# Two sparse convolutions on one core: gathers and sums written out item by item

## The chip, the cores and the metric

One core of one Trainium2 chip runs one program. The metric is the device time of an execution in microseconds; the time before is the median of three runs.

## The reference, cut to what matters

Four blocks act one after the other on x, 6250 nodes of 256 float32 features, each added to x behind a layer norm: a sum over 106,250 weighted edges, a mixture of eight experts, a graph network of two convolutions, and a feed-forward block over selected tokens. The change touches the two convolutions only:

```python
def _gcn_conv(x, src, dst, W, b):
    ones = jnp.ones((src.shape[0],), x.dtype)
    deg_out = jnp.maximum(segment_sum(ones, src, num_segments=N), 1.0)
    deg_in = jnp.maximum(segment_sum(ones, dst, num_segments=N), 1.0)
    h = x * (deg_out ** (-0.5))[:, None]
    h = h @ W
    m = segment_sum(h[src], dst, num_segments=N)
    return m * (deg_in ** (-0.5))[:, None] + b
h = _gcn_conv(x, src, dst, W1, b1)
h = relu(h)
h = _gcn_conv(h, src, dst, W2, b2)
h = _layer_norm(h, gamma, beta)
```

The edges come sorted by their target dst. All tensors are float32.

## The kernel before, in words

**Tiles.** The nodes lie in T = 49 tiles of 128. The edges are cut into NI = 880 items of up to 128 edges whose targets all lie in one tile of nodes. For each item three tables in SBUF hold a column of 128 entries: SRCI the source rows, DREL the place of each target within its tile, and (in the first stage) weights. The array `rows` holds for each item the column in `reg_b` at which its tile's sums begin. A convolution first sums the gathered rows and only then multiplies by W, tile by tile.

**One item of a convolution.** (1) POOL issues an indirect DMA that gathers 128 rows of 256 features from DRAM (`conv_rows` in the profile) into a slot of a ring of U = 16 in `work` (L535, in `gathers`). (2) DVE compares IOTA, a row of 0 to 127, with the item's column of DREL and so writes a one-hot matrix of 128x128 (L1153, in `item_sums`). (3) PE multiplies the one-hot by the gathered rows and a column of ones into a PSUM bank, 257 columns: the sums over the targets, and their number (L1617, in `item_products`). (4) DVE adds the bank to the accumulator in `reg_b`, at a column that comes from a register (L1165).

**The rings.** The slot of a gather is free when the matmul sixteen items back is done: POOL waits on `p1_mm` (`p2_mm` in the second pass). There are four one-hots and four banks. DVE makes the one-hot of item i+2 in front of the accumulation of item i; PE waits for the accumulation of item i-4 before it writes its bank again. Each gather counts up `ring_dma0` to `ring_dma15`.

**Index columns.** POOL doesn't read its index column from the table. ACT copies eight columns at a time to the staging array STG (L685, in `staging`), when the eight gathers before them in those slots have landed, and POOL waits for this copy once in eight gathers. Before each gather POOL increments a semaphore `turn` and waits for `const`.

**Loops.** All four engines run over the items in a hardware loop of 16 items a round, with the first round written out; what they wait for is a register plus a constant. DVE loads the offsets of four items into registers at a time (L257, in `load_offsets`) and computes further addresses in its sequencer (the profile's DVEq).

**The order around the passes.** The engines work in the order of their own programs and meet at semaphores. Before the first pass stands the mixture of experts (L1482 is one of its matmuls), after it the products with W1: PE transposes and multiplies each tile (L1520 in `tile_products`), DVE scales it and adds the bias (L1285, in `product`), ACT applies the relu, SP writes the rows out, and the second pass begins. POOL, behind its last gather of the first pass, adds a row of constants to all of X (L567, 128x12544 elements), and then turns to the second pass. DVE, behind its last accumulation of a pass, takes a maximum and inverse roots of the counts before the first `product`.

**Other lines that the rows name.** L468: eight gathers of edge blocks at the start, one behind the other with no wait between them, the index columns in an array `small`. L481: the scatter of the first stage's messages, in a loop of 880. L889 and L1019: tensor_tensor compares of two SBUF operands in other stages. L977: a one-hot of the first stage, the same form as L1153.

Of the kernel before, what the change touches and what calls it, by code (L numbers as in the profile page):

```python
# [14 lines left out]
P = 128  # L15
ALU = mybir.AluOpType
# [37 lines left out]
def gnn_program(nc, x, src, dst, edge_weight, Wr, br, ln_g, ln_b, W1, b1, W2, b2,  # L54
# [31 lines left out]
    with ExitStack() as ctx:  # L86
# [77 lines left out]

        G, OH, OHT = carve(0, U * W, 4 * P, 2 * P)
# [47 lines left out]
        STG, PIDX = sm(U).bitcast(I32), sm(U).bitcast(I32)  # L213
# [125 lines left out]
        def _(sp):  # L339
# [72 lines left out]
            sp.wait_ge(z("p2_add"), NI + 1)  # L412
            sp.wait_ge(z("p2_stg"), NI)
# [18 lines left out]
        def _(pool):  # L432
# [91 lines left out]
            def gathers(tag, table):  # L524

                def body(i0, first):
                    for u in range(U):
                        if u % 8 == 0:
                            pool.wait_ge(z(f"{tag}_stg"), i0 + u + 8)
                        if not first:  # L530
                            pool.wait_ge(z(f"{tag}_mm"), i0 + u + 1 - U)
                        if u % 8 == 0 or not first:
                            pool.sem_inc(z("turn"), 1)
                        pool.wait_ge(z("const"), CONST)
                        g.indirect_dma_start(G[:, u, 0:D], None, table,  # L535
                                             bass.IndirectOffsetOnAxis(ap=STG[:, u:u + 1], axis=0)
                                             ).then_inc(z(f"ring_dma{u}"), 16)
                body(0, True)
                with pool.Fori(U, NI, U) as i0:
                    body(i0, False)  # L540
# [49 lines left out]
        def _(act):  # L590
# [87 lines left out]
            def staging(tag):  # L678

                def body(i0, first):  # L680
                    for h in range(0, U, 8):
                        if not first:
                            for u in range(h, h + 8):
                                act.wait_ge(z(f"ring_dma{u}"), i0 + BEFORE[tag])
                        a.copy(STG[:, h:h + 8], SRCI[:, bass.ds(i0 + h, 8)]).then_inc(z(f"{tag}_stg"), 8)  # L685
                body(0, True)
                with act.Fori(U, NI, U) as i0:
                    body(i0, False)

# [33 lines left out]
            staging("p1")  # L723
# [11 lines left out]
            staging("p2")  # L735
# [23 lines left out]
        def _(v):  # L759
# [390 lines left out]
            def item_sums(tag):  # L1150

                def onehot(i, j):
# [3 lines left out]
                def body(i0):  # L1156
                    for u in range(U):
                        i = i0 + u
                        if u % 4 == 0:
                            offs = load_offsets(DVE_, ROW_D, i, (T - 1) * (D + 1))  # L1160
# [533 lines left out]
```

## Time and profile before

| what | value |
| --- | --- |
| time, median of 3 runs | 5863.63 us (5860.67 to 5864.42) |
| the profiled execution: span | 6669.2 us |
| instructions in it | 93083 |
| items of the two passes | 2 x 880 |

The profile comes from one execution that was recorded by the hardware profiler; its own time is its span, and it is longer than the timed executions, which run without a recording. PE is TensorE's matmuls, PEld its weight loads, DVE VectorE, ACT ScalarE, POOL GpSimd, SP SyncE. A name ending in q is the sequencer of that engine: register arithmetic, branches and register loads are put there and are not counted as busy time. PEclk is the clock that the throttle granted to TensorE, as a share of 2.4 GHz.

### The profile page before, as it was taken

Reading aid. Unit: us, or ns where it says so; the run is one execution under the profiler, and the core shown is the slowest. Engines: PE = TensorE matmul, PEld = TensorE weight load, DVE = VectorE, ACT = ScalarE, POOL = GpSimd, SP = SyncE. Lnnn points to the kernel's source line nnn. Section 1 sums busy time; section 2 is a strip of 40 time slices with the busy share of each in tenths; the row PEclk is TensorE's granted clock in tenths of the full one; section 3 lists DMA queues with packets and bytes.
Section 4 is the critical chain, followed back from the end, with each engine's and each line's share of the span. In section 5 each row is a group of like instructions: output and inputs, shape, how many; then the busy total and the mean of one; then the engine's idle time right before and its main releaser. Section 6 shows DMA issues by size and latency. Waiting matters only on the chain. (4 is left out here: it accounts for less than half of the span.)

```text
span 6669.2 us, 93083 instructions
## 1 busy us (share of the span) xinstructions
PE 4350.5 (65%) x15535; PEld 2796.3 (42%) x15536; DVE 3245.9 (49%) x12513; ACT 1175.7 (18%) x3960; POOL 3014.1 (45%) x2954
## 2 busy tenths in 40 slices
PE   1667677777677759999945555555555555555459
PEld 0444444444455446666633233332333323323346
DVE  7555555555566664333334444444544444444662
ACT  4333333333000053222220000000110000000322
POOL 0555555555000012333336666666546666666412
PEclk9777677667999959999976766666776776676769
DMA  2122222222666651221243333333232333333211
GB/s 69 70 75 72 73 74 75 74 73 73 183 186 188 178 179 25 33 33 33 33 121 87 86 87 88 87 87 87 70 94 87 88 88 88 87 87 88 72 41 31
DMA packets 287945, 575.13 MB, mean 86 GB/s; under 512 B 57794, under 2 KB 138307, under 8 KB 287758
## 3 DMA queue, kind: packets, MB, share of 16 engines
q0 software_dynamic: 152576, 376.72, 19.9%
q1 hardware_dynamic: 101902, 136.46, 6.5%
q10 hardware_dynamic: 33408, 61.31, 3.3%
q8 instruction: 19, 0.31, 0.0%
q14 instruction: 40, 0.33, 0.0%
HBM read 408.39 MB, written 173.72 MB: 87 GB/s over the span
## 5 line engine op out<-in xcount | busy, mean ns | idle before, releaser
L1617 PE MATMUL bank<-work 128*128 128x257 f32 x3520 | 1453.6, 552 | 1283.1 <-DVE work L1153 727.1
L535 POOL DMA_INDIRECT work<-conv_rows,small x1760 | 1666.2, 947 | 1088.0 <-issue 417.9
L1617 PEld LDWEIGHTS bank<-work 128*128 128x128 f32 x3520 | 806.2, 261 | 1930.6 <-DVE work L1153 921.5
L1165 DVE TENSOR_TENSOR reg_b<-reg_b,bank 128x257 f32 x1760 | 743.2, 422 | 915.6 <-issue 435.6
L481 POOL DMA_INDIRECT messages<-work,small x880 | 857.4, 974 | 687.6 <-DVE small L998 258.4
L1482 PE MATMUL bank<-reg_b,work 128*128 x1760 | 885.8, 598 | 4.3 <-ACT work L627 0.5
L1153 DVE TENSOR_SCALAR work<-iota,tables 128x128 f32<-128x128 f32 x1764 | 556.2, 316 | 623.4 <-issue 577.8
L1498 PE MATMUL bank<-work,reg_b 128*128 128x257 f32 x1856 | 474.6, 408 | 192.5 <-DVE reg_b L1019 192.4
L685 ACT COPY small<-tables 128x8 int32 (+1 forms) x220 | 43.2, 197 | 2557.2 <-DMA work<-conv_rows,small 2377.8
L637 ACT COPY work<-bank 128x256 f32<-128x256 f32 x880 | 329.1, 374 | 909.5 <-PE bank L1482 526.6
L1498 PEld LDWEIGHTS bank<-work,reg_b 128*128 128x128 f32 x1856 | 332.0, 196 | 335.5 <-issue 283.1
L1461 PE MATMUL bank<-small,trib 128*128 128x49 bf16 x1761 | 229.9, 215 | 348.0 <-DVE small L993 317.1
L993 DVE SCALAR_TENSOR_TENSOR small<-bank,small 128x49 f32<-128x49 f32 x880 | 184.9, 210 | 501.1 <-remote 385.6
L1461 PEld LDWEIGHTS bank<-small,trib 128*128 128x128 bf16 x1761 | 201.8, 128 | 523.8 <-DVE small L993 375.8
L665 ACT ACTIVATE work<-bank,param_t 128x128 f32<-128x128 f32 x1056 | 286.5, 382 | 753.2 <-PE bank L1564 753.1
L1482 PEld LDWEIGHTS bank<-reg_b,work 128*128 128x128 f32 x1760 | 384.0, 271 | 26.4 <-issue 10.1
L1556 PE MATMUL bank<-reg_b,work 128*128 x1696 | 385.5, 381 | 2.5 <-ACT work L665 2.5
L1546 PE MATMUL bank<-reg_a,work 128*128 x848 | 383.4, 595 | 1.1 <-DVE work L1093 1.1
L1452 PE MATMUL bank<-ident,work 128*128 128x128 f32 x881 | 322.9, 367 | 90.3 <-issue 60.1
L496 POOL DMA_INDIRECT work<-expert_in_rows,work x106 | 104.4, 985 | 555.8 <-DVE work L1085 537.1
L977 DVE TENSOR_SCALAR work<-iota,tables 128x128 f32<-128x128 f32 x881 | 321.1, 365 | 26.8 <-issue 20.2
L1556 PEld LDWEIGHTS bank<-reg_b,work 128*128 128x128 f32 x1696 | 315.2, 191 | 42.3 <-issue 3.5
(297 smaller groups left out, 4566.3 us busy)
## 6 DMA issues: line engine op xcount, KB each, us to landing
work<-messages SPq DMA_DIRECT2D x232, 258.0 KB, 3.0
work<-messages ACTq DMA_DIRECT2D x232, 258.0 KB, 3.3
work<-conv_rows,small POOLq DMA_INDIRECT x1760
messages<-work,small POOLq DMA_INDIRECT x880
conv_rows<-work SPq DMA_DIRECT2D x14, 896.0 KB, 4.1
reg_a<-in_L_ffn_W_dram SPq DMA_DIRECT2D x8, 1024.0 KB, 12.7
reg_b<-in_L_ffn_W_dram SPq DMA_DIRECT2D x8, 1024.0 KB, 12.2
residual_rows<-reg_a SPq DMA_DIRECT2D x7, 896.0 KB, 4.6
```

Of the source, the lines that this page charges most:

```text
L481: g.indirect_dma_start(msgs, bass.IndirectOffsetOnAxis(ap=PIDX[:, u:u + 1], axis=0), G[:, u, :], None, bounds_check=E - 1, oob_is_err=Fals ...
L535: g.indirect_dma_start(G[:, u, 0:D], None, table, bass.IndirectOffsetOnAxis(ap=STG[:, u:u + 1], axis=0)).then_inc(z(f"ring_dma{u}"), 16)
L637: a.copy(G[:, u, 0:D], ps[3 + u % 2][:, 0:D]).then_inc(z("m_row"), 1)
L1153: v.tensor_scalar(OH[:, j % 4, :], IOTA[:], DREL[:, bass.ds(i, 1)], None, ALU.is_equal).then_inc(z(f"{tag}_oh"), 1)
L1165: v.tensor_tensor(acc, acc, ps[u % 4][:, 0:D + 1], ALU.add).then_inc(z(f"{tag}_add"), 1)
L1452: pe.transpose(ps[j % 2][:, 0:P], OH[:, j % 4, :], IDENT[:]).then_inc(z("m_tr"), 1)
L1461: ins = pe.matmul(ps[2][:, 0:T], TRIB[:, which, :], BOH[:, j % 4, 0:T], start=False, stop=False, skip_group_check=True)
L1482: pe.matmul(ps[3 + u % 2][:, 0:D], OHT[:, u % 2, :], XNf[:, bass.ds(offs[u % 4], D)], start=True, stop=True).then_inc(z("m_mm"), 1)
L1498: pe.matmul(ps[u // 2 % 4][:, 0:D + 1], SOH[:, u % 8, :], G[:, u, 0:D + 1], start=(u % 2 == 0), stop=(u % 2 == 1)).then_inc(z("s_mm"), 1)
L1546: ins = pe.matmul(ps[1 + h // 512][:, :], XE[:, s, c, :], w_, start=(c == 0), stop=(c == KC - 1))
L1556: ins = pe.matmul(ps[5 + s][:, 0:D], HTS[:, k, :], w_, start=(k == 0), stop=(k == HC - 1))
L1617: pe.matmul(ps[u % 4][:, 0:D + 1], OH[:, u % 4, :], G[:, u, 0:D + 1], start=True, stop=True).then_inc(z(f"{tag}_mm"), 1)
```

## The change

Only the two convolution passes change.

- POOL: the gathers of all 880 items are written out, with constants in place of registers. The index column is read from the table SRCI; there is no staging array, no `turn`, and no wait for `const`.
- ACT: the copies to the staging array are gone.
- DVE: the one-hots of four items are made by one tensor_tensor (IOTA repeated four times against four columns of DREL, each repeated over 128 elements) into a ring of eight one-hots, which lies in a part of `reg_a`. Those of items i+4 to i+7 stand in front of the accumulation of item i, where i is a multiple of four. Registers are loaded for sixteen items at a time. All items are written out.
- PE: all items are written out; eight banks in place of four; it waits once in four items for one-hots, and for the accumulation eight items back.
- The count `p1_add` starts at 0 in place of 1, so waits for its end ask for NI.

```diff
--- before.py
+++ after.py
@@ -162,6 +162,8 @@
         HID, HIS = (a_.bitcast(BF16) for a_ in (HIB[:, 0:EC // 2], HIB[:, EC // 2:EC]))
         CMPD, CMPS = CMPD.bitcast(BF16), CMPS.bitcast(BF16)
 
+        OHN = 4
+        OHP = ta[:, 0:2 * OHN * P].rearrange("p (s n) -> p s n", n=P)
         G, OH, OHT = carve(0, U * W, 4 * P, 2 * P)
         G = G.rearrange("p (u w) -> p u w", w=W)
         OH = OH.rearrange("p (s n) -> p s n", s=4)
@@ -210,7 +212,7 @@
             taken[0] += n
             return small[:, taken[0] - n:taken[0]]
         BOH = sm(4 * 26).bitcast(BF16).rearrange("p (s n) -> p s n", s=4)
-        STG, PIDX = sm(U).bitcast(I32), sm(U).bitcast(I32)
+        PIDX = sm(U).bitcast(I32)
         POS, JUNK = sm(4), sm(64)
         CNT = sm(104)
         ZERO = sm(2 * NT)
@@ -409,8 +411,7 @@
                 sp.wait_ge(z("relu1"), (c + 1) * CH)
                 sp.dma_start(nodes(conv2_t, c), XR[:, c % 2, :, :]).then_inc(z(f"rows_out{c % 2}"), 16)
 
-            sp.wait_ge(z("p2_add"), NI + 1)
-            sp.wait_ge(z("p2_stg"), NI)
+            sp.wait_ge(z("p2_add"), NI)
             sp.dma_start(fw1s[:, :, :], fw1.rearrange("(c p) h -> p c h", p=P)).then_inc(z("fw_in"), 16)
             sp.dma_start(fw2s[:, :, :], fw2.rearrange("(c p) d -> p c d", p=P)).then_inc(z("fw_in"), 16)
 
@@ -523,21 +524,13 @@
 
             def gathers(tag, table):
 
-                def body(i0, first):
-                    for u in range(U):
-                        if u % 8 == 0:
-                            pool.wait_ge(z(f"{tag}_stg"), i0 + u + 8)
-                        if not first:
-                            pool.wait_ge(z(f"{tag}_mm"), i0 + u + 1 - U)
-                        if u % 8 == 0 or not first:
-                            pool.sem_inc(z("turn"), 1)
-                        pool.wait_ge(z("const"), CONST)
-                        g.indirect_dma_start(G[:, u, 0:D], None, table,
-                                             bass.IndirectOffsetOnAxis(ap=STG[:, u:u + 1], axis=0)
-                                             ).then_inc(z(f"ring_dma{u}"), 16)
-                body(0, True)
-                with pool.Fori(U, NI, U) as i0:
-                    body(i0, False)
+                for i in range(NI):
+                    u = i % U
+                    if i >= U:
+                        pool.wait_ge(z(f"{tag}_mm"), i + 1 - U)
+                    g.indirect_dma_start(G[:, u, 0:D], None, table,
+                                         bass.IndirectOffsetOnAxis(ap=SRCI[:, i:i + 1], axis=0)
+                                         ).then_inc(z(f"ring_dma{u}"), 16)
 
             def chunk(c):
                 w_ = slice(c * CH, (c + 1) * CH)
@@ -674,18 +667,6 @@
                 with act.Fori(2, tiles, 2) as j0:
                     for s in range(2):
                         hidden(j0 + s, e_(j0 + s), False)
-
-            def staging(tag):
-
-                def body(i0, first):
-                    for h in range(0, U, 8):
-                        if not first:
-                            for u in range(h, h + 8):
-                                act.wait_ge(z(f"ring_dma{u}"), i0 + BEFORE[tag])
-                        a.copy(STG[:, h:h + 8], SRCI[:, bass.ds(i0 + h, 8)]).then_inc(z(f"{tag}_stg"), 8)
-                body(0, True)
-                with act.Fori(U, NI, U) as i0:
-                    body(i0, False)
 
             def evacuate(tag, t):
 
@@ -720,7 +701,6 @@
                     if c >= 3:
                         act.wait_ge(*rows_out((c - 1) % 2, 1, (c - 1) // 2))
                     ln_apply("ln3", c - 1, lambda i: X[:, (c - 1) * CH + i, :], lambda i: XR[:, (c - 1) % 2, i, :])
-            staging("p1")
             inv_root("di", RM)
             evacuate("c1", 0)
             for t in range(T):
@@ -732,7 +712,6 @@
                     act.wait_ge(*rows_out(c % 2, 2, c // 2))
                 a.activation(XR[:, c % 2, t % CH, :], ZB[:, t % 2, :], ACT.Relu, scale=DO[:, t:t + 1]
                              ).then_inc(z("relu1"), 1)
-            staging("p2")
 
             evacuate("c2", 0)
             for t in range(T):
@@ -1149,28 +1128,26 @@
 
             def item_sums(tag):
 
-                def onehot(i, j):
-                    v.tensor_scalar(OH[:, j % 4, :], IOTA[:], DREL[:, bass.ds(i, 1)], None, ALU.is_equal
-                                    ).then_inc(z(f"{tag}_oh"), 1)
-
-                def body(i0):
-                    for u in range(U):
-                        i = i0 + u
-                        if u % 4 == 0:
-                            offs = load_offsets(DVE_, ROW_D, i, (T - 1) * (D + 1))
-                        onehot(i + 2, u + 2)
-                        v.wait_ge(z(f"{tag}_add"), i + 1)
-                        v.wait_ge(z(f"{tag}_mm"), i + 1)
-                        acc = ACCf[:, bass.ds(offs[u % 4], D + 1)]
-                        v.tensor_tensor(acc, acc, ps[u % 4][:, 0:D + 1], ALU.add).then_inc(z(f"{tag}_add"), 1)
-                step(v.memset(G[:, :, D:D + 1], 1.0))
-                onehot(0, 0)
-                onehot(1, 1)
-                v.engine_nop().then_inc(z(f"{tag}_add"), 1)
-                with v.Fori(0, NI - U, U) as i0:
-                    body(i0)
-                body(NI - U)
-
+                def onehots(i):
+                    if i >= 2 * OHN:
+                        v.wait_ge(z(f"{tag}_mm"), i - OHN)
+                    v.tensor_tensor(OHP[:, i % (2 * OHN):i % (2 * OHN) + OHN, :],
+                                    IOTA[:].rearrange("p (o n) -> p o n", o=1).to_broadcast([P, OHN, P]),
+                                    DREL[:, i:i + OHN].rearrange("p (s o) -> p s o", o=1).to_broadcast([P, OHN, P]),
+                                    ALU.is_equal).then_inc(z(f"{tag}_oh"), OHN)
+
+                v.memset(G[:, :, D:D + 1], 1.0).then_inc(z(f"{tag}_one"), 1)
+                onehots(0)
+                for i in range(NI):
+                    if i % U == 0:
+                        offs = load_offsets(DVE_, ROW_D, i, (T - 1) * (D + 1), U)
+                    if i % OHN == 0 and i + OHN < NI:
+                        onehots(i + OHN)
+                    v.wait_ge(z(f"{tag}_mm"), i + 1)
+                    if i:
+                        v.wait_ge(z(f"{tag}_add"), i)
+                    acc = ACCf[:, bass.ds(offs[i % U], D + 1)]
+                    v.tensor_tensor(acc, acc, ps[i % 8][:, 0:D + 1], ALU.add).then_inc(z(f"{tag}_add"), 1)
 
             v.wait_ge(z("s_add"), NIS + 1)
             step(v.tensor_scalar(DI, ACC[:, :, D], 1.0, None, ALU.max))
@@ -1274,7 +1251,7 @@
                 v.wait_ge(*rows_out(k, 1))
             v.engine_nop().then_inc(z("conv_ready"), 1)
             item_sums("p1")
-            v.wait_ge(z("p1_add"), NI + 1)
+            v.wait_ge(z("p1_add"), NI)
             step(v.tensor_scalar(RM, ACC[:, :, D], 1.0, None, ALU.max))
             inv_root("di", DI, RM)
 
@@ -1293,7 +1270,7 @@
             v.wait_ge(z("acc2_zero"), 1)
             v.engine_nop().then_inc(z("conv_ready"), 1)
             item_sums("p2")
-            v.wait_ge(z("p2_add"), NI + 1)
+            v.wait_ge(z("p2_add"), NI)
 
             for t in range(T):
                 product("c2", 1, t, ACC[:, t, 0:D], GB2B).then_inc(z("lin2"), 1)
@@ -1607,18 +1584,17 @@
                               stop=(n == steps - 1), skip_group_check=True).then_inc(z(f"{tag}_inv"), 1)
 
             def item_products(tag):
-                def body(i0, first):
-                    for u in range(U):
-                        i = i0 + u
-                        pe.wait_ge(z(f"{tag}_oh"), i + 1)
-                        pe.wait_ge(z(f"ring_dma{u}"), i0 + (16 + BEFORE[tag]))
-                        if not (first and u < 4):
-                            pe.wait_ge(z(f"{tag}_add"), i - 2)
-                        pe.matmul(ps[u % 4][:, 0:D + 1], OH[:, u % 4, :], G[:, u, 0:D + 1], start=True, stop=True
-                                  ).then_inc(z(f"{tag}_mm"), 1)
-                body(0, True)
-                with pe.Fori(U, NI, U) as i0:
-                    body(i0, False)
+
+                pe.wait_ge(z(f"{tag}_one"), 1)
+                for i in range(NI):
+                    u = i % U
+                    if i % OHN == 0:
+                        pe.wait_ge(z(f"{tag}_oh"), i + OHN)
+                    pe.wait_ge(z(f"ring_dma{u}"), 16 * (i // U + 1) + BEFORE[tag])
+                    if i >= 8:
+                        pe.wait_ge(z(f"{tag}_add"), i - 7)
+                    pe.matmul(ps[i % 8][:, 0:D + 1], OHP[:, i % (2 * OHN), :], G[:, u, 0:D + 1], start=True, stop=True
+                              ).then_inc(z(f"{tag}_mm"), 1)
 
 
             pe.wait_ge(z("par_in"), PAR_IN)
@@ -1641,14 +1617,14 @@
             pe.wait_ge(z("conv_ready"), 1)
             item_products("p1")
             pe.wait_ge(z("tail_in"), 8 * 16)
-            pe.wait_ge(z("p1_add"), NI + 1)
+            pe.wait_ge(z("p1_add"), NI)
             for t in range(T):
                 if t >= 4:
                     pe.wait_ge(z("lin1"), t - 3)
                 tile_products("c1", t, D, lambda c: gws[:, 0, c, :], 2 + t % 4, 0)
             pe.wait_ge(z("conv_ready"), 2)
             item_products("p2")
-            pe.wait_ge(z("p2_add"), NI + 1)
+            pe.wait_ge(z("p2_add"), NI)
             for t in range(T):
                 if t >= 4:
                     pe.wait_ge(z("lin2"), t - 3)
```

## Rows read from the trace of the kernel before

**Rows 1.** Page, part 1: busy time, share and instructions of each engine.

```profile
PE 4350.5 (65%) x15535; PEld 2796.3 (42%) x15536; DVE 3245.9 (49%) x12513; ACT 1175.7 (18%) x3960; POOL 3014.1 (45%) x2954
```

**Rows 2.** Stages: stretch, us; busy PE, PEld, DVE, ACT, POOL; clock; DMA; GB/s.

```profile
2525.00:3400.00 875.00, 860.27 (x3638) 596.12 (x3636) 314.77 (x882) 241.05 (x881) 271.42 (x212) 0.99 0.20 32
...
3454.00:4772.00 1318.00, 719.99 (x1738) 399.46 (x1738) 545.68 (x1735) 21.32 (x108) 832.52 (x880) 0.68 0.30 87
```

**Rows 3.** Page, part 5: costliest groups; busy, mean ns; idle before.

```profile
L535 POOL DMA_INDIRECT work<-conv_rows,small x1760 | 1666.2, 947 | 1088.0 <-issue 417.9
...
L481 POOL DMA_INDIRECT messages<-work,small x880 | 857.4, 974 | 687.6 <-DVE small L998 258.4
...
L1153 DVE TENSOR_SCALAR work<-iota,tables 128x128 f32<-128x128 f32 x1764 | 556.2, 316 | 623.4 <-issue 577.8
```

**Rows 4.** Timeline of POOL: start, duration (us), instruction, wait before it.

```profile
3454.46 1.03 POOL L535 DMA_INDIRECT work<-conv_rows,small  x1 [42.38 <-DMA conv_rows<-work]
...
3455.79 0.99 POOL L535 DMA_INDIRECT work<-conv_rows,small  x1 [0.30 <-issue]
...
4627.01 0.94 POOL L535 DMA_INDIRECT work<-conv_rows,small  x1 [3.34 <-PE bank L1617]
...
4771.35 0.94 POOL L535 DMA_INDIRECT work<-conv_rows,small  x1 [0.30 <-issue]
...
4772.31 22.41 POOL L567 TENSOR_TENSOR reg_a<-reg_a,reg_b 128x12544 f32<-128x12544 f32 x1
...
4874.39 0.96 POOL L535 DMA_INDIRECT work<-conv_rows,small  x1 [79.66 <-DMA conv_rows<-work]
...
6187.77 0.95 POOL L535 DMA_INDIRECT work<-conv_rows,small  x1 [0.30 <-issue]
```

**Rows 5.** Timeline of DVE inside the first pass.

```profile
4617.80 0.42 DVE L1165 TENSOR_TENSOR reg_b<-reg_b,bank 128x257 f32 x1 [0.35 <-PE bank L1617]
...
4626.42 0.42 DVE L1165 TENSOR_TENSOR reg_b<-reg_b,bank 128x257 f32 x1 [2.70 <-PE bank L1617]
```

**Rows 6.** DVE's sequencer at L1153, two stretches: least, median, most ns.

```profile
L1153 DVEq FUSED_REGOPS  x11: 64/64/102, 4608.1 to 4616.8; - x11
...
L1153 DVEq FUSED_REGOPS  x2: 700/712/724, 4621.9 to 4625.5; - x2
```

**Rows 7.** Timeline of POOL at the start.

```profile
118.67 2.01 POOL L468 DMA_INDIRECT reg_b<-edge_blocks,small  x1 [0.30 <-issue]
```

**Rows 8.** Single lines: count, then least, median, most ns, and when.

```profile
L1019 DVE TENSOR_TENSOR reg_b<-iota,small x464: 426/427/430, 1677.8 to 2332.4; 128x256 f32<-128x256 f32 x155
...
L889 DVE TENSOR_TENSOR reg_a<-ident,small x5: 1202/1203/1226, 112.3 to 148.3; 128x1024 f32<-128x1024 f32 x5
...
L257 DVEq TENSOR_LOAD <-rows x110: 1823/1828/1874, 1701.3 to 2318.4; - x110
...
L1617 PE MATMUL bank<-work x3520: 377/602/797, 3457.4 to 6197.1; 128*128 128x257 f32 x196
```

**Rows 9.** Timeline of DVE at the start of the first pass.

```profile
3460.43 0.28 DVE L1153 TENSOR_SCALAR work<-iota,tables 128x128 f32<-128x128 f32 x1
```

**Rows 10.** Timeline of DVE at the start.

```profile
118.65 1.20 DVE L889 TENSOR_TENSOR reg_a<-ident,small 128x1024 f32<-128x1024 f32 x1
```

**Rows 11.** Timeline of POOL and DVE in the message stage.

```profile
1403.24 1.04 POOL L481 DMA_INDIRECT messages<-work,small  x1 [0.30 <-DVE small L998]
...
1403.09 0.34 DVE L977 TENSOR_SCALAR work<-iota,tables 128x128 f32<-128x128 f32 x1
```

**Rows 12.** Timeline of DVE at the ends of the passes.

```profile
4772.96 0.42 DVE L1165 TENSOR_TENSOR reg_b<-reg_b,bank 128x257 f32 x1 [1.82 <-PE bank L1617]
...
4773.30 21.52 DVE L1153 TENSOR_SCALAR work<-iota,tables 128x128 f32<-128x128 f32 x1
...
4806.51 0.48 DVE L1285 SCALAR_TENSOR_TENSOR work<-bank,small,reg_b 128x256 f32<-128x256 f32 x1 [0.27 <-PE bank L1520]
...
6197.77 0.42 DVE L1165 TENSOR_TENSOR reg_b<-reg_b,bank 128x257 f32 x1
```

## The prediction

> **What bounds the kernel now.** I read the page first, then the stages one by one. The page shows a program of several stages in which no engine is busy throughout: PE 65%, DVE 49%, POOL 45% [rows 1]. The table by stage says where the change can act: the first convolution takes 1318 us, the second as long, and in the first PE is busy 720 us at a granted clock of 0.68, DVE 546, POOL 833, ACT 21 [rows 2]. The expert stage beside them has PE busy 860 of 875 us at clock 0.99 and isn't touched.
>
> The costliest groups give the work of one item of a convolution: one gather of 947 ns on POOL and one one-hot of 316 ns on DVE [rows 3], beside an accumulation of 0.42 us. None fills the 1.50 us that an item takes. POOL's own rows explain that. A gather follows the one before after 0.30 us whenever nothing holds it, so 1.25 us from start to start, and now and then POOL stops, here for 3.34 us, until a matmul has freed its slot [rows 4]. The passes run from their first gather to their last in 1316.9 and 1313.4 us [rows 4]; 879 steps of 1.25 us are 1098.8 us. So POOL's pace is 2198 us of the two, and the stops are 433 us.
>
> What stops POOL stands in DVE's rows of the same microseconds: from 4617.8 to 4626.4 DVE starts three accumulations of 0.42 us, the first and the last of them shown [rows 5], and its own sequencer instructions (register additions before a one-hot), 64 ns in the microseconds before, take 700 to 724 ns each [rows 6]. PE then waits for a one-hot and POOL for PE's matmul, whose end frees the slot.
>
> **POOL, part by part.** The semaphore increment, the wait for constants and the register arithmetic in front of each gather go. The eight gathers at L468 have nothing in front of them and still stand 0.30 us apart, as the one shown [rows 7]; so 1.25 us is the gather's own pace and this saves 0 us (from below, too: fewer instructions can't lengthen it; a written-out list costs at most what L468 shows). Reading the index column from the table instead of the staged copy: the nearest rows are the gathers at L468, whose index column lies in another place of the same kind, with the same 0.30 us, so 0. ACT's copies disappear, 21 us of its 1318 [rows 2]; POOL waits for one of them only before every eighth gather, and the copy is due as soon as the eight transfers of the round before have landed, so 0; what is late next in its place is the matmul fifteen items back, as now.
>
> **PE.** Waits on constants instead of registers and eight banks instead of four. PE is in use for 0.82 us per item [rows 2], under POOL's 1.25: 0 while POOL sets the pace; without that cover PE would have 0.43 us to spare per item.
>
> **DVE.** Four one-hots become one tensor_tensor of 128x512 with two operands in SBUF. That form stands in the trace: 427 ns for 256 columns, 1203 ns for 1024 [rows 8], so 1.01 ns a column and 0.69 us for 512, against 4 x 0.316 = 1.26 us. The offsets come 16 at a time instead of 4: 8 take DVE 1828 ns [rows 8], 0.23 us each, so 16 take about 3.6 us once in 16 items, the same per item (0.23). DVE needs 0.17 + 0.42 + 0.23 = 0.82 us per item instead of 0.97, both under 1.25. A pause of 3.6 us is three gathers; the ring holds 16 and item 1 was through DVE 4.6 us after its gather's start [rows 4, 9], so it is hidden. Fewer sequencer instructions per item (three or four instead of five) shorten the slow stretches where they occur.
>
> **The new cost.** POOL and DVE block each other in this trace. At L468 one gather of eight takes 2.01 us, where the median is 0.95. It started at 118.67, 0.02 us after a DVE tensor_tensor with two SBUF operands that ran until 119.85 [rows 7, 10]: 1.18 us were left, the gather got 1.06 longer. At 1403.24 a scatter took 1.04 us, where the mean is 0.97 [rows 3], while a one-hot had 0.19 us left [rows 11]. Both fit one reading: a gather that starts while such a DVE instruction runs is longer by what that has left, less 0.12 us. Today's one-hot of 0.28 us can add 0.16 us at most, and the mean gather of the passes is 947 ns [rows 3]: nothing. The new one lasts 0.69 us, 440 times. It starts right behind the accumulation of the item before: for item 1 that was 4.64 us after its gather's start [rows 4, 9], which is 0.89 us after a later gather's start, so it ends at 1.58, with the next gather at 1.25: 0.33 left, 0.21 added. At the low of PE's two clock levels, that is; at the high one a matmul takes 377 instead of 797 ns [rows 8], a pair of them and all behind it come about 0.6 us sooner, and nothing collides. A mean clock of 0.68 [rows 2] is 64% of the low level: 440 x 0.21 x 0.64 = 59 us. With no fixed phase the mean is 0.57 x 0.57 / (2 x 1.25) = 0.13 us, 57 us in all. Ends: 0 and 440 x 0.57 = 250 us. I take 55, where both readings meet.
>
> The Trainium skill, "SBUF — State Buffer", section "Who interferes with whom", says that a tensor_tensor with both inputs in SBUF contends with GpSimd's reads, but infers that it does not hold up descriptor generation, which needs the write side. The row at 118.67 speaks against that inference; by it the new cost would be 0 and the time 5841 us (the second case below).
>
> **The ends of the passes.** After the last gather of pass 1 POOL adds beta for 22.4 us, and DVE's next one-hot takes 21.5 us instead of 0.28: it gets through only when POOL is done [rows 4, 12]. The items still due follow, and the first product comes at 4806.5 [rows 12]. Afterwards the last one-hots are made eight items earlier and an accumulation passes beside POOL (0.42 us at 4772.96 [rows 12]). The maximum and the roots may still wait for POOL, and take about 2.3 us: 4794.7 + 2.3 = 4797.0, 9.5 us saved. Pass 2's last accumulation starts 10.0 us after its last gather [rows 4, 12], where 4.3 would do (4.64 less the 0.34 between accumulation and one-hot): 5.7. Together 15 us where DVE lags as in the profile, 2.5 where it doesn't; I take 8.
>
> **The sum and the timed runs.** In the profiled execution: 6669.2 - 15 + 55 and minus whatever of the 433 us goes; I expect half, so about 6490. The timed median, 5863.6, is 805.6 us below that span. The expert stage (875 us, PE-bound) can't be shorter without the recording, and to find 805.6 us outside it and the convolutions, the remaining 3161 us would have to shrink by 25%. So at least part of the 433 us, and I think nearly all, is absent from the timed runs: the stretched sequencer instructions look like time that the recording costs. Bounds for the stops in the timed runs: 0 and 433; I take 15, near the lower. Timed: 5863.6 - 15 (stops) - 8 (ends) + 55 (collisions) = **5896 us**.
>
> **Rivals.**
> 1. *Collisions, as above*, 0.42: 5896, its own range 5865 to 5985.
> 2. *No collisions*, 0.26: the phase misses, or one long gather proves little. For it: the page's inference, and that one long gather is one. Against it: two separate places give the same 0.12 us. 5863.6 - 15 - 8 = 5841, half of the time inside the bound of no change.
> 3. *The stops are real in the timed runs and go*, 0.20; faster. Place: DVE's slow stretches. For it: they take 433 us of the profiled span, one-hots four at a time and eight banks let DVE and PE run ahead, and the sequencer has fewer instructions to be slow in. Against it: the 805.6 us above. Price: half of the stops real 5863.6 - 217 - 8 + 55 = 5694, all of them 5471. It decides as soon as more than 47 us of stops go.
> 4. *The slow stretches stay and the longer register load lands in them*, 0.12: then each load that falls into one (8.6 us of the 20 us that 16 gathers take, so 43% of 110) holds DVE, and so POOL, between 0 and 3.6 us longer; at the middle 47 x 1.8 = 85 us: 5981. This is also the case in which the change doesn't do what it says.
>
> **Numbers.** Range 5660 to 5985: cases 1, 2 and 4, and case 3 up to 250 us of real stops (5863.6 - 250 - 8 + 55). A difference under 0.2% (12 us) counts as none. Faster: nearly all of case 3 and half of case 2, 0.31. Same: half of case 2 and the low end of case 1, 0.23. Slower: 0.46.
>
> **What the profile afterwards would show.** Gathers with a mean above 0.97 us and some hundred between 1.0 and 1.5, each begun beside a 0.69 us tensor_tensor (case 1), or 0.946 throughout (case 2). The step from gather to gather still 1.25 us where nothing interferes; a shorter step would make the POOL part wrong. 440 one-hots of 0.69 us; register loads of 3.6 us with no stop of POOL behind them (else case 4). Stops of POOL below 220 us in sum; a time far below 5800 would mean that I was wrong to ascribe them to the recording. Pass 1's beta addition with accumulations done within 6 us of its start.

## The result, and the profile after

The changed kernel takes 5895.44 us (median of 4 runs, 5883.44 to 5898.29), the kernel before in the same session 5864.02 (5860.67 to 5866.95): ratio 1.0050, 95% interval 1.0038 to 1.0063. It is slower by 31 us; 5896 was forecast. The profiled execution is one of the four, 5883.44 us with a span of 5881.8.

Part 1 of the page of the changed kernel, and of its part 5 the groups of an item (line, engine, operation; busy us, mean ns):

```profile
PE 4671.4 (79%) x15535; PEld 2711.5 (46%) x15536; DVE 3117.7 (53%) x11189; ACT 1142.5 (19%) x3740; POOL 3045.6 (52%) x2954
...
L1596 PE MATMUL bank<-work,reg_a 128*128 128x257 f32 x3520 | 1920.6, 655 | 382.0 <-DMA work<-conv_rows,tables 222.7
L531 POOL DMA_INDIRECT work<-conv_rows,tables x1760 | 1695.1, 963 | 648.4 <-issue 419.6
...
L1150 DVE TENSOR_TENSOR reg_b<-reg_b,bank 128x257 f32 x1760 | 742.0, 422 | 870.1 <-PE bank L1596 802.7
...
L1134 DVE TENSOR_TENSOR reg_a<-iota,tables 128x512 f32<-128x512 f32 x440 | 302.1, 686 | 375.1 <-PE bank L1596 305.7
```

Its first convolution in the table by stage (the columns of [rows 2]):

```profile
3080.00:4195.00 1115.00, 965.05 (x1755) 411.36 (x1756) 497.30 (x1098) 0.00 (x0) 846.61 (x880) 0.59 0.36 104
```

Its timeline of POOL: the first gather, two neighbours inside the pass, the last gather, the addition, and the second pass (start, duration in us):

```profile
3080.55 1.48 POOL L531 DMA_INDIRECT work<-conv_rows,tables  x1 [41.47 <-DMA conv_rows<-work]
...
3301.24 0.95 POOL L531 DMA_INDIRECT work<-conv_rows,tables  x1 [0.30 <-issue]
3302.49 1.35 POOL L531 DMA_INDIRECT work<-conv_rows,tables  x1 [0.30 <-issue]
...
4194.29 0.95 POOL L531 DMA_INDIRECT work<-conv_rows,tables  x1 [0.30 <-issue]
4195.26 22.41 POOL L560 TENSOR_TENSOR reg_a<-reg_a,reg_b 128x12544 f32<-128x12544 f32 x1
4288.92 0.96 POOL L531 DMA_INDIRECT work<-conv_rows,tables  x1 [71.25 <-DMA conv_rows<-work]
...
5404.00 0.95 POOL L531 DMA_INDIRECT work<-conv_rows,tables  x1 [0.30 <-issue]
```

And of DVE, beside the long gather and at the ends of the passes:

```profile
3302.34 0.68 DVE L1134 TENSOR_TENSOR reg_a<-iota,tables 128x512 f32<-128x512 f32 x1
...
4199.73 0.42 DVE L1150 TENSOR_TENSOR reg_b<-reg_b,bank 128x257 f32 x1 [1.23 <-PE bank L1596]
4200.19 17.55 DVE L1255 TENSOR_SCALAR small<-reg_b 128x49 f32<-128x49 f32 x1
...
4220.60 0.48 DVE L1262 SCALAR_TENSOR_TENSOR work<-bank,small,reg_b 128x256 f32<-128x256 f32 x1 [1.08 <-PE bank L1497]
...
5409.66 0.42 DVE L1150 TENSOR_TENSOR reg_b<-reg_b,bank 128x257 f32 x1 [1.60 <-PE bank L1596]
```

The passes now run from first to last gather in 1113.7 and 1115.1 us. Against [rows 4] that looks like 400 us won, and the spans like 787 (6669.2 to 5881.8), while the timed runs say 31 us lost. So the profile before can't be set against this one as it stands. Within this one the reader sees three things. POOL no longer stops: inside a pass all gathers follow 0.30 us behind the one before. The mean gather has grown from 947 to 963 ns [rows 3]. The gather at 3302.49 takes 1.35 us; it started while the one-hot of 3302.34 had 0.54 us left (0.684 us long), and it is 0.41 us longer than 0.946. Such a meeting, a gather that starts while a DVE instruction still runs and gets longer by it, is called a collision below; the phase of a one-hot is how long after a gather's start it starts itself.

### The profile page after: what moved, and what is told of

It reads as the page before. It is cut to its first block and busy times, and to the rows that moved or that the text cites. A ratio compares the mean times of both kernels' runs of the same rounds, so it can differ in the third digit from the quotient of the medians.

```text
span 5881.8 us, 81790 instructions
## 1 busy us (share of the span) xinstructions
PE 4671.4 (79%) x15535; PEld 2711.5 (46%) x15536; DVE 3117.7 (53%) x11189; ACT 1142.5 (19%) x3740; POOL 3045.6 (52%) x2954
## 5 line engine op out<-in xcount | busy, mean ns | idle before, releaser
L1596 PE MATMUL bank<-work,reg_a 128*128 128x257 f32 x3520 | 1920.6, 655 | 382.0 <-DMA work<-conv_rows,tables 222.7
L531 POOL DMA_INDIRECT work<-conv_rows,tables x1760 | 1695.1, 963 | 648.4 <-issue 419.6
L1596 PEld LDWEIGHTS bank<-work,reg_a 128*128 128x128 f32 x3520 | 824.9, 288 | 1477.0 <-DMA work<-conv_rows,tables 1038.0
L1459 PE MATMUL bank<-reg_b,work 128*128 x1760 | 736.0, 506 | 0.4
L1134 DVE TENSOR_TENSOR reg_a<-iota,tables 128x512 f32<-128x512 f32 x440 | 302.1, 686 | 375.1 <-PE bank L1596 305.7
L1429 PE MATMUL bank<-ident,work 128*128 128x128 f32 x881 | 283.7, 322 | 171.9 <-DVE work L956 89.0
L1533 PE MATMUL bank<-reg_b,work 128*128 x1696 | 383.8, 379 | 2.5 <-ACT work L658 2.5
L956 DVE TENSOR_SCALAR work<-iota,tables 128x128 f32<-128x128 f32 x881 | 329.4, 374 | 26.4 <-issue 23.1
L1459 PEld LDWEIGHTS bank<-reg_b,work 128*128 128x128 f32 x1760 | 319.9, 227 | 32.1 <-issue 0.2
L1533 PEld LDWEIGHTS bank<-reg_b,work 128*128 128x128 f32 x1696 | 314.0, 190 | 41.8 <-issue 3.5
L1082 DVE COPY work<-bank 128x512 f32<-128x512 f32 x132 | 91.4, 692 | 422.1 <-PE bank L1523 422.1
L1429 PEld LDWEIGHTS bank<-ident,work 128*128 128x128 f32 x881 | 141.8, 161 | 342.9 <-DVE work L956 209.8
```

What stands on the lines that cost most here:

```text
L531: g.indirect_dma_start(G[:, u, 0:D], None, table, bass.IndirectOffsetOnAxis(ap=SRCI[:, i:i + 1], axis=0)).then_inc(z(f"ring_dma{u}"), 16)
L956: v.tensor_scalar(OH[:, j % 4, :], IOTA[:], DREL[:, bass.ds(i, 1)], WT[:, bass.ds(i, 1)], ALU.is_equal, ALU.mult).then_inc(z("m_oh"), 1)
L1134: v.tensor_tensor(OHP[:, i % (2 * OHN):i % (2 * OHN) + OHN, :], IOTA[:].rearrange("p (o n) -> p o n", o=1).to_broadcast([P, OHN, P]), DREL ...
L1429: pe.transpose(ps[j % 2][:, 0:P], OH[:, j % 4, :], IDENT[:]).then_inc(z("m_tr"), 1)
L1459: pe.matmul(ps[3 + u % 2][:, 0:D], OHT[:, u % 2, :], XNf[:, bass.ds(offs[u % 4], D)], start=True, stop=True).then_inc(z("m_mm"), 1)
L1533: ins = pe.matmul(ps[5 + s][:, 0:D], HTS[:, k, :], w_, start=(k == 0), stop=(k == HC - 1))
```

## Experiments

Each was timed beside the kernel before on one chip. The last column is POOL's busy time in the 1760 gathers less the 1664.9 us that they take in a profile of the kernel before without stops (e11, below). Up to 5 us of it are no collision. In the profiles of e1, e2, e3, e5 and e7 the median gather takes 0.949 us, in the others 0.946 or 0.947; e5 is the changed kernel again, so the 3 ns belong to the execution and not to an edit. In e1 three of 1760 gathers take more than 1.0 us.

| run | us | ratio to before, 95% interval | gathers beyond 1664.9 us |
| --- | --- | --- | --- |
| changed | 5895.4 | 1.0050 (1.0038 to 1.0063) | 30.2 |
| e1 POOL and ACT part only | 5860.2 | 0.9998 (0.9989 to 1.0007) | 5.1 |
| e2 four tensor_scalar one-hots | 5861.3 | 1.0002 (0.9993 to 1.0011) | 8.5 |
| e3 four at once, in loops | 5881.7 | 1.0035 (1.0023 to 1.0048) | 29.4 |
| e4 eight at once | 5950.2 | 1.0153 (1.0139 to 1.0167) | 90.8 |
| e5 changed, again | 5892.9 | 1.0055 (1.0041 to 1.0069) | 38.3 |
| e6 one-hots wait for a landing | 5876.3 | 1.0026 (1.0017 to 1.0035) | 25.0 |
| e7 changed, addition on DVE | 5870.9 | 1.0016 (1.0007 to 1.0025) | 38.5 |
| e8 e2 and e7 together | 5845.3 | 0.9972 (0.9962 to 0.9983) | 4.2 |
| e9 e6 with loads of four | 5861.8 | 1.0004 (0.9994 to 1.0013) | 6.1 |
| e10 changed, loads of four | 5886.3 | 1.0043 (1.0029 to 1.0057) | 27.4 |
| e11 before, again | 5860.6 | 0.9999 (0.9989 to 1.0008) | 0 |
| e12 before, addition on DVE | 5839.6 | 0.9963 (0.9950 to 0.9977) | 0.1 |

**The kernel before, once more (e11).**

> The kernel before, run and profiled once more. Theory (the slow stretches of DVE's sequencer and POOL's stops behind them, 433 us, are made by recording and aren't in the timed runs): the timed runs at 5861, and either the profiled execution is again some 800 us above them, with stops, or it has none this time and passes of 1102 us each at a span near 5860. Rival (the stops are in the timed runs too): a profile without them would be some 430 us below the timed runs.

This profile has a span of 5860.8 us (its own time 5862.45). Its page, its first convolution by stage, and the two parts of L1153, the second the additions in DVE's sequencer (least, median, most ns):

```profile
PE 4717.4 (80%) x15535; PEld 2719.9 (46%) x15536; DVE 3221.5 (55%) x12513; ACT 1190.1 (20%) x3960; POOL 3012.8 (51%) x2954
...
L535 POOL DMA_INDIRECT work<-conv_rows,small x1760 | 1664.9, 946 | 653.2 <-issue 490.0
```

```profile
3084.00:4184.00 1100.00, 963.30 (x1755) 408.10 (x1756) 551.73 (x1753) 21.33 (x108) 832.26 (x880) 0.58 0.37 105
```

```profile
L1153 DVE TENSOR_SCALAR work<-iota,tables x1764: 274/280/23217, 3083.5 to 5385.2; 128x128 f32<-128x128 f32 x196
L1153 DVEq FUSED_REGOPS  x1728: 57/64/64, 3084.7 to 5363.4; - x192
```

None of the 1728 sequencer instructions takes more than 64 ns, where [rows 6] had 700 and more. The end of the first pass, on POOL and on DVE:

```profile
4183.33 0.95 POOL L535 DMA_INDIRECT work<-conv_rows,small  x1 [0.30 <-issue]
4184.30 22.41 POOL L567 TENSOR_TENSOR reg_a<-reg_a,reg_b 128x12544 f32<-128x12544 f32 x1
4281.80 0.96 POOL L535 DMA_INDIRECT work<-conv_rows,small  x1 [75.09 <-DMA conv_rows<-work]
```

```profile
4183.59 23.22 DVE L1153 TENSOR_SCALAR work<-iota,tables 128x128 f32<-128x128 f32 x1 [0.60 <-issue]
...
4213.06 0.48 DVE L1285 SCALAR_TENSOR_TENSOR work<-bank,small,reg_b 128x256 f32<-128x256 f32 x1 [1.46 <-PE bank L1520]
```

The passes take 1099.3 and 1099.1 us: POOL's own pace, without a stop. So the 433 us of stops were in that one recorded execution; that the timed ones have none follows from their times, which are those of e11. Of the 808 us between the two spans 432 lie in the passes and 370 before them. What made that recording slow stays open; this one, recorded in the same way, isn't. From here on this is the profile of before. Set against it the changed kernel's differs so: passes +30.4 us; from the last gather of the first to the first gather of the second 94.6 in place of 98.5, -3.8; before the passes -3.5; behind them -2.1; in sum the 21.0 us between the two spans.

**One part alone (e1, e2, e3).** e1 takes the diff of `gathers` and drops `staging`, and leaves DVE and PE as before. e2 changes one instruction of the changed kernel:

```diff
-                    v.tensor_tensor(OHP[:, i % (2 * OHN):i % (2 * OHN) + OHN, :], ...
+                    for k in range(OHN):
+                        v.tensor_scalar(OHP[:, i % (2 * OHN) + k, :], IOTA[:], DREL[:, i + k:i + k + 1], None,
+                                        ALU.is_equal).then_inc(z(f"{tag}_oh"), 1)
```

e3 puts the tensor_tensor of four one-hots and the eight banks into the loops of the kernel before.

> Before, with only POOL's and ACT's part of the change: gathers written out, index column from the table, no staging; one-hots, banks and DVE's and PE's loops as before. Theory (the whole extra time of the change is 128x512 one-hots that hold up gathers, 30 us in the profile after; the written-out gathers cost and save nothing): 5864 us within 5, gathers 0.946 us with none above 1.1. Rival (the written-out gather list or the column read from the table costs the 31 us): 5895. Rival (removing increments and waits saves time on POOL): below 5850.

> The changed kernel with each group of four one-hots made by four tensor_scalar instructions (0.28 us, one SBUF operand of 128 columns each) in place of one tensor_tensor of 128x512; all else as changed. Theory (collisions): the 30 us go, 5865 us, or up to 9 us less, as the ends of the passes gain what the profile after shows; gathers mean 0.946. Rival (written-out code, or constant waits, cost): stays at 5895. Rival (DVE's longer time per item matters): above 5895.

> Before, with only the one-hots of four items at once and eight banks, DVE and PE still in loops, offsets still four at a time, POOL and ACT as before. Theory (collisions): 5895 us within 10, with some hundred long gathers, each longer by what is left of the one-hot less 0.127 us. Rival (writing out costs): 5864.

The one-hots and gathers on the page of e2, and the gathers of e3:

```profile
L531 POOL DMA_INDIRECT work<-conv_rows,tables x1760 | 1673.4, 951 | 649.0 <-issue 419.4
...
L1135 DVE TENSOR_SCALAR reg_a<-iota,tables 128x128 f32<-128x128 f32 x1760 | 390.8, 298 | 366.7 <-PE bank L1595 305.1
```

```profile
L537 POOL DMA_INDIRECT work<-conv_rows,small x1760 | 1694.3, 963 | 651.1 <-issue 497.8
```

e1 and e2 lie within 1 us of the kernel before (e2's gathers take 8.5 us more, and the stretch from pass to pass 3.4 less); e3, which has nothing written out but a first and a last round, has the long gathers (mean 963 ns, as the changed kernel) and 21 us of the loss. That settles what costs: the 128x512 tensor_tensor. The written-out lists, the constant waits and the column read from the table cost and save nothing that can be measured. It doesn't settle whether the length or the two operands in SBUF do it, since e2 takes away both at once.

Two fences of e2, POOL and then DVE, show that the one-operand form collides too:

```profile
5179.58 1.04 POOL L531 DMA_INDIRECT work<-conv_rows,tables  x1 [0.30 <-issue]
```

```profile
5178.94 0.87 DVE L1135 TENSOR_SCALAR reg_a<-iota,tables 128x128 f32<-128x128 f32 x4
```

The last of the four tensor_scalar one-hots runs from 5179.524 to 5179.803: 0.22 us were left at the gather's start, and the gather is 0.09 us longer than 0.949. In e2 85 gathers that began with more than 0.15 us of such a one-hot left got longer (the first gather of a pass left out), by the rest less 0.129 us in the middle, which is the same rule as for the tensor_tensor; in sum it makes 3.9 us. In e11 22 gathers did, for 1.0 us in sum. None was lengthened by more than 0.1 us; these one-hots are 0.28 us long.

e3 came out 13 us under its expectation. Its profiled execution, at 5887.16 us, is 25 above e11's with 29.4 of gather time.

**Its size (e4).** One number, `OHN = 8`.

> The changed kernel with the one-hots of eight items at once (128x1024, about 1.20 us, 220 times) and a ring of sixteen. Theory: with the starting phases that the profile after shows (middle 0.66 us behind a gather's start) a one-hot leaves 0.66 + 1.20 - 1.25 = 0.61 us over the next gather's start, so 0.48 us are added about 220 x 2 / 2 = 220 times a pass-pair: some 100 us in place of 30, 5965 us (range 5930 to 6000). Rival (a cost per one-hot instruction, which are halved): 5880. Rival (written-out code): 5895.

The two groups on its page, then one gather and, in the next fence, the one-hot beside it:

```profile
L531 POOL DMA_INDIRECT work<-conv_rows,tables x1760 | 1755.7, 998 | 648.8 <-issue 419.4
...
L1134 DVE TENSOR_TENSOR reg_a<-iota,tables 128x1024 f32<-128x1024 f32 x220 | 268.9, 1222 | 373.1 <-PE bank L1596 338.1
```

```profile
3309.41 1.54 POOL L531 DMA_INDIRECT work<-conv_rows,tables  x1 [0.30 <-issue]
```

```profile
3308.91 1.22 DVE L1134 TENSOR_TENSOR reg_a<-iota,tables 128x1024 f32<-128x1024 f32 x1
```

Half as many one-hots, less DVE time in sum (269 for 302 us), and 90.8 us of added gather time, as 215 of the 220 have more than 0.15 us left over a gather's start; the kernel is 89.9 us above the one before. 5965 was expected, 5950 measured. The one-hot above had 0.72 us left at 3309.41; the gather got 0.59 us longer.

**Its phase (e5, e6, e9, e10).** e5 is the changed kernel again. e6 adds a wait in front of the one-hots:

```diff
                     if i % OHN == 0 and i + OHN < NI:
+                        n = i + 1
+                        v.wait_ge(z(f"ring_dma{n % U}"), 16 * (n // U + 1) + BEFORE[tag])
                         onehots(i + OHN)
```

e9 is e6, and e10 the changed kernel, with `load_offsets` for four items instead of sixteen.

> The changed kernel once more, beside the next three. Its first four timed runs lay between 5883 and 5898 us and its profile at 5882; with the clean spans of the two kernels without collisions at 5862 to 5863, theory (collisions of 29 us in the profile) expects 5885 to 5895 and about 65 long gathers a pass. Rival (the timed runs hold 10 us more that the profile doesn't show): 5895 again with a span of 5882.

> The changed kernel with one wait more on DVE: the 128x512 one-hot in front of accumulation i also waits until gather i+1 has landed. In the profile after, a matmul that waits for its gather starts 2.75 to 2.85 us behind that gather's start, so 0.25 to 0.35 us behind a later gather's start; a one-hot of 0.68 us begun there ends at about 1.0, before the next gather at 1.25. Theory (only the phase decides): collisions gone with the same 440 instructions of the same length, 5862 us within 4, gathers mean 0.950. Rival (a long tensor_tensor costs POOL something wherever it stands, or the written-out code costs): as the changed kernel, 5885 to 5895. Rival (the added wait delays accumulations): above that.

> As e6_phase, with the offsets loaded four at a time, as before the change, in place of sixteen. In e6_phase the one-hots of items 16n and 16n+12 made 8 collisions for 2.2 us, those of items 16n+4 and 16n+8, which come right behind the 3.6 us load of sixteen offsets and the accumulations held up by it, 75 for 23.6 us. Theory (only the phase decides, and the load had displaced it): under 5 us of collisions left, 5862 us within 4. Rival (the wait on the landing doesn't set the phase, or four shorter loads displace as much as a long one): 5870 to 5880 as e6_phase.

> The changed kernel with the offsets loaded four at a time; no other edit. In the profile after, all four groups of a round collide, those away from the load too (13.1 of 29.7 us, at a middle phase of 0.71 us). Theory (the phase behind an accumulation makes collisions by itself): some 15 to 30 us stay, 5878 to 5895 us. Rival (the long load is the whole cause): 5862.

Gathers on the pages of e6, e9 and e10, and what ended DVE's idle time before the one-hots in e9:

```profile
L531 POOL DMA_INDIRECT work<-conv_rows,tables x1760 | 1689.9, 960 | 647.8 <-issue 411.8
```

```profile
L531 POOL DMA_INDIRECT work<-conv_rows,tables x1760 | 1671.0, 949 | 648.2 <-issue 425.2
```

```profile
L531 POOL DMA_INDIRECT work<-conv_rows,tables x1760 | 1692.3, 962 | 649.9 <-issue 436.6
```

```profile
L1134 DVE TENSOR_TENSOR reg_a<-iota,tables x440: 691/693/755, 3079.8 to 5373.8; 128x512 f32<-128x512 f32 x147
...
  DMA work<-conv_rows,tables: 233.5, 234
```

e6 missed its 5862: the wait set the phase of the one-hots of items 16n and 16n+12 only (8 collisions in 220). The others start behind the load of sixteen offsets (median 3.59 us, the row further on) and the accumulations that it held up, when the landing is long past. e9 shortens the load, and with the same 440 tensor_tensor of 0.69 us the time is that of the kernel before: 5861.8. They still add 6 us of gather time, which the 4.5 us that it gains from pass to pass nearly make up. e10 has the short loads without the wait: 27 us stay. So the same number of instructions of the same length costs 6 us or 27; what costs is the part of them that lies over a gather's start. Without the wait the 440 one-hots make 98 (e10) to 145 (e5) gathers of more than 1.0 us, with it and the short loads 29 (e9).

e5's profiled execution took 5902.90 us, its others 5889 to 5900. Of the 19.5 us between its span (5901.3) and that of the first profile 8.1 are gather time (3.5 of them from a median gather of 949 in place of 947 ns), the rest lies outside the passes. The time varies from execution to execution: the changed kernel's nine runs spread over 19 us, those of the kernel before on one chip over some 8 to 11.

The register load of the changed kernel (least, median, most ns):

```profile
L259 DVEq TENSOR_LOAD <-rows x110: 3581/3590/3609, 3080.5 to 5386.8; - x110
```

**The addition on POOL (e7, e8, e12).** The line at L567 of the kernel before goes, and DVE gets one instruction in the loop of products:

```diff
-            g.tensor_tensor(X, X, per_column(BETB, T), ALU.add).then_inc(z("beta_in"), 1)
...
                 product("c1", 0, t, ZB[:, t % 2, :], GB1B).then_inc(z("lin1"), 1)
+                v.tensor_tensor(X[:, t, :], X[:, t, :], BETB, ALU.add).then_inc(z("beta_in"), 1)
```

> The changed kernel with POOL's 22.4 us addition behind pass 1 taken off POOL: DVE adds the row to one tile of X (128x256, 0.43 us, two SBUF operands) behind each of the 49 products, where it idles 0.6 to 0.9 us a tile. Theory (the addition locks DVE's maximum for 17.5 us at the end of pass 1): from the last accumulation to the first product about 4.5 us in place of 20.9, so 16 us less than the changed kernel in the same session. Rival (something else ends there anyway, such as rows or tail parameters, or the added DVE work slows the products): within 5 us of the changed kernel.

> Both repairs: four tensor_scalar one-hots per group (as in e2_ts_onehots) and the addition on DVE (as in e7_beta_on_dve); else the changed kernel. If both are independent: 5861 - 16 = 5845 us, faster than the kernel before by 0.27% and than the changed one by some 45 us. If the addition doesn't matter: 5861.

> The kernel before with one edit: POOL's 22.4 us addition behind pass 1 goes to DVE, one tile of 256 columns behind each of the 49 products (as in e7_beta_on_dve and e8_ts_and_beta). In the clean profile of the kernel before it holds the last one-hots for 23.2 us, and from the last gather of pass 1 to the first of pass 2 pass 98.5 us; with the addition moved e8_ts_and_beta has 78.5. Theory: 20 us less, 5841 us (range 5838 to 5847), so nothing of the change is needed for the fastest version. Rival (the shortening needs the written-out passes, where all one-hots are done before the addition): 5850 or more.

The last gather of pass 1 and the first of pass 2 in e12, then its DVE at that place:

```profile
4183.31 0.95 POOL L535 DMA_INDIRECT work<-conv_rows,small  x1 [0.30 <-issue]
4261.13 0.94 POOL L535 DMA_INDIRECT work<-conv_rows,small  x1 [76.88 <-DMA conv_rows<-work]
```

```profile
4188.62 0.42 DVE L1162 TENSOR_TENSOR reg_b<-reg_b,bank 128x257 f32 x1 [0.71 <-PE bank L1615]
4189.07 0.20 DVE L1275 TENSOR_SCALAR small<-reg_b 128x49 f32<-128x49 f32 x1
...
4192.53 0.48 DVE L1282 SCALAR_TENSOR_TENSOR work<-bank,small,reg_b 128x256 f32<-128x256 f32 x1 [1.46 <-PE bank L1518]
4192.93 0.42 DVE L1287 TENSOR_TENSOR reg_a<-reg_a,reg_b 128x256 f32<-128x256 f32 x1
```

From pass to pass 77.8 us instead of 98.5. The one-hot that e11 shows held for 23.22 us isn't held any more, and the maximum, 17.55 us long beside the addition in the changed kernel, takes 0.20. e7 gained 22 us on e5 (16 expected), e8 reached its 5845, and e12, the kernel before with this edit alone, is the fastest: 5839.6 us, 22 us under the kernel before beside it and, by the ratios, some 50 under the changed one. Of the 5.7 us between e8 and e12 4.1 are gather time.

## Why the prediction was right, and where only the sum was

**Right.** POOL sets the pace; 1.25 us is the gather's own (1.250 to 1.251 us a step in e11 and e12, so 1099 a pass; 1098.8 was worked out). The cover over PE is thinner than I read from [rows 2]: in e11 PE is in use for 963 us of a pass, 1.09 us per item and not 0.82, which leaves it 0.16 us and not 0.43. The POOL part is worth 0 (e1). The stops belong to one recorded execution: I put 15 of 433 us into the timed runs; e11 shows none, and e1, which leaves DVE's program as it was, is equal to before within 0.1%. Rival 3 falls (its price for all of the stops should read 5478 by the sum as given, not 5471), and rival 4 with it: the load of sixteen takes the 3.6 us foreseen, and no gather in the profile after waits more than 0.35 us for anything.

The rule of the collision held better than its two rows promised. Of the 179 gathers that began with more than 0.15 us of a one-hot left, the added time was that rest less 0.127 us in the middle, and less 0.124 to 0.131 in eight of ten (0.12 was read from two). Two of them, begun within 0.02 us of the one-hot's start, took no harm, and the one-hot grew by 0.04 to 0.06 us instead; for the tensor_scalar one-hots of e2 this is so up to 0.08 us behind their start, so that the 0.16 us that I took as the most one could add was 0.09. Rival 2 falls. The Trainium skill, "SBUF — State Buffer", section "Who interferes with whom", reports a probe in which a tensor_tensor did not stall DMAs, and infers that descriptor generation needs the write side, which it doesn't take. In this trace 177 of those 179 gathers were held up.

**Mis-sized.** The steps of the sum that failed are its terms for collisions, stops and ends: all three were off, and their errors nearly cancelled; that 5896 lies half a microsecond from the median is partly luck, as the executions themselves differ by 19 us:

| term | forecast, us | profiles show |
| --- | --- | --- |
| collisions | +55 | +30 (e5: 38, of which 5 are the 3 ns on every gather) |
| ends of the passes | -8 | -3.8 at the first, 0 at the second |
| stops in the timed runs | -15 | 0 |
| sum | +32 | +26; the spans differ from e11's by +21 and (e5) +40; timed +31.4 |

Between the +26 and the spans stand the stretches before and behind the passes, -5.6 us in the first profile and +5.5 in e5; no edit explains them.

The step on collisions failed twice in its detail. The phase: I carried item 1's accumulation (0.89 us behind a gather's start) over to all one-hots; they spread over the period, about half of them at 0.6 to 0.9 us. And the clock: "at the high one nothing collides" is wrong. Of the 90 one-hots that began when the matmul started last was one of less than 460 ns, 32 made a long gather, 8.4 us in sum. The granted clock in the pass was 0.59, and not 0.68 [rows 2]; e11, the same program as in [rows 2] without the stops, has 0.58, with PE busy 963 of 1100 us in place of 720 of 1318. With 0.59 the first reading would have given 440 x 0.21 x 0.82 = 76 us, still further off; that the two readings met near 55 was chance. With no phase assumed the second reading gave 57 us, twice what was found. The phases aren't spread evenly: e6 shows that the one-hots behind the load and the others have phases of their own. Why they lie so that half of the 57 us comes out isn't worked out.

The ends: in e11 DVE doesn't lag as in [rows 12], so the case of 2.5 us was the one that held. From the last gather of pass 1 to the first product pass 29.7 us in e11 and 26.3 after, 3.4 less; pass 2's last accumulation starts 5.5 us behind its last gather in e11 and 5.7 after, where [rows 4, 12] had 10.0, so nothing was to be had there. I took 8, between the two. What I saw there and didn't follow up, POOL's addition that locks DVE for 22 us, was worth 22 us (e12), the most of anything tried.

## What to carry to other kernels

Where GpSimd's gathers set the pace, look at what of a VectorE instruction lies over the next gather's start: that is what it costs here, not its own length. Keep such instructions short (the 0.28 us tensor_scalar added 0.09 us at most), or anchor them to an event with a known phase, and don't make them longer by merging. Whether a tensor_scalar of 0.69 us would have cost less than the tensor_tensor of 0.69 us was not run. Don't make GpSimd do a long elementwise pass where VectorE's next small step ends a stage. And set a profile's span beside the timed runs first: where they are as far apart as the 800 us here, stops seen in it have to be found in a second profile before they are worth a change.

## What the runs showed of the hardware

- VectorE and GpSimd hold each other up, both ways. A gather is held by the rest of a 0.68 us tensor_tensor less 0.127 us, and by the rest of a 0.28 us tensor_scalar less 0.129 us (e2). A 22.4 us GpSimd tensor_tensor holds a VectorE tensor_scalar over 49 columns for 17.55 us and a one-hot for 23.2 us.
- A gather holds a tensor_scalar too: in e11 the 152 one-hots that began 0.45 to 0.55 us behind a gather's start took 0.50 us in the middle, where the median of all is 0.28.
- Accumulations with one operand in PSUM didn't lengthen a gather: 352 gathers of the changed kernel began during one and beside no one-hot, and their mean is 946 ns. Three accumulations ran in 0.42 us each beside the 22.4 us addition.
- The load of sixteen registers takes 3.59 us, of four 0.95: 0.22 and 0.24 us each.
- One recording of the same program can be 800 us slower than its timed runs and another not at all (6669.2 and 5860.8 us of span); why isn't known.
